# The first layer's weights loaded under the attention, and a new order of the layers' first group and of the change of layers

## The chip, the cores and the metric

One core of one Trainium2 chip runs the whole program. The metric is the device time in microseconds of one execution, the median of the runs shown.

## The reference, cut to what matters

```
mod = silu(c) @ wmod                      -> sa, ca, ga, sb, cb, gb (4 batches, 256 each)
h = layernorm(x) * (1 + ca) + sa          # x: 4 x 1024 x 256
x = x + ga * attention(h)                 # 4 heads of 64, full attention, RMS norm of q and k
h = layernorm(x) * (1 + cb) + sb
for l in range(2):                        # "the layers", weights of their own
    s = shift_token(h)                    # second half of the features from the token before
    q, k, v = split(s @ wqkv[l])          # 8 heads of 64
    q, k = l2norm(q) * q_scale[l], l2norm(k) * k_scale[l]
    q, k = rotary(q, k)
    h = h + local_attention(q, k, v) @ wo[l]     # windows of 128, own and previous
    a, g = split(layernorm(shift_token(h)) @ w1[l] + b1[l])
    h = h + (a * gelu(g)) @ w2[l] + b2[l]
x = x + gb * h
```

All products of weights are done in three passes over a high and a low part (the helper of lines 260 to 262), so each weight has to be split after it is loaded: the high part is a copy to the matmul's format on ScalarE (ACT), the low part is the difference of raw and high.

## The kernel before

Three blocks follow each other with a barrier between them: setup, attention, layers. In each block every engine has its own instruction list, written out by hand, and engines wait for each other on semaphores that count finished steps.

In the layers a unit is 128 tokens, a group g is four units; groups 0 to 7 are the first layer, 8 to 15 the second. The lists run over g from -1. In group -1 only the projections of group 0 are made. In every other group there are 12 rounds r of attention of two heads each (scores on TensorE, `minima` L1528 on VectorE (DVE), `exps` L1337 on ACT, `inverse` L1536 on DVE, `probabilities` L1737 on GpSimd (POOL), transposes and values on TensorE), and then 16 slots k. A slot holds the rest of the attention, one product of `qkv` for the group after (k 0 to 11), the feed-forward's `hidden` from k 4 and `outputs` from k 10. For the group after, ACT takes `squares` L1319, DVE `sums` L1495, the chain of 12 small instructions `norms` (L1501 and L89 to L94) and `rotated` (L1512, L1514), POOL `trig` (L1725 twice, L1730), which multiplies q and k with the table of angles `tab`. A product writes one of the banks P, A0 to A3; the scores use A0 to A3 as well.

Start of the layers: SyncE issues, after the barrier, the rows of units 0 and 1, `wqkv`, the rows of units 2 and 3, `tab`, six small loads of the scales, `w2`, `wo`, `w1`, the mask and `b2` (L1921 to L1933). The raw weights land in tiles that are free until the first group needs them. `first_wqkv`, `first_w2_wo` and `first_w1` are the splits. The low part of `w2` and `wo` is made on POOL in slot 5 of group -1, that of `w1` on DVE in slot 7, just ahead of the norms of units 0 and 1 in slot 8. POOL multiplies `tab` by the scales (L1711) first.

Change of layers: in group 7 SyncE's `take_q` loads the second layer's `wqkv` in six pieces of 256 KB into `ge`, `up`, `xn`, `base` (four, then two once the first two are split), and then `tab` and the scales again. In group 8 `take_rest` loads two pieces of `wo`, six of `w1` and three of `w2`, each batch after a wait for the splits of the last; the stores of group 7 and the shifts of group 8 stand behind it in the same queue. ACT makes the high parts in the rounds that W_Q, W_O and W_1 name (L1403, L1408, L1415), `piece_2` in slot 0; POOL makes the low parts of `wqkv`, `wo` and `w2` (L1771, L1775, L1781), DVE that of `w1` (L1618). The group's `moments` (L1551) need the shifted row, a transfer from SBUF to SBUF by SyncE (`shift`, L1844).

## Time and profile before

| | us |
|---|---|
| median of 3 runs | 2210.22 (2209.44 to 2210.82) |
| the profiled execution | 2207.61 |
| its span, first to last instruction | 2205.8 |
| attention's last stores, then first issue of the layers | 664.9 |
| busy: TensorE 1865.4 (85%), VectorE 1510.0 (68%), ScalarE 1186.2 (54%), GpSimd 996.6 (45%) | |

The span is the time from the first to the last instruction; the execution's own time is 1.8 us more, and the median of the runs 2.6 us above that. A busy share is an average over three blocks: what a stage is worth is read in its own stretch.

### The profile page before, as it was taken

Reading aid. Unit: us, or ns where it says so; the run is one execution under the profiler, and the core shown is the slowest. Engines: PE = TensorE matmul, PEld = TensorE weight load, DVE = VectorE, ACT = ScalarE, POOL = GpSimd, SP = SyncE. Lnnn points to the kernel's source line nnn. Section 1 sums busy time; section 2 is a strip of 40 time slices with the busy share of each in tenths; the row PEclk is TensorE's granted clock in tenths of the full one; section 3 lists DMA queues with packets and bytes.
Section 4 is the critical chain, followed back from the end, with each engine's and each line's share of the span. In section 5 each row is a group of like instructions: output and inputs, shape, how many; then the busy total and the mean of one; then the engine's idle time right before and its main releaser. Section 6 shows DMA issues by size and latency. Waiting matters only on the chain.

```text
span 2205.8 us, 36469 instructions
## 1 busy us (share of the span) xinstructions
PE 1865.4 (85%) x12941; PEld 1403.2 (64%) x12941; DVE 1510.0 (68%) x3723; ACT 1186.2 (54%) x2717; POOL 996.6 (45%) x788
## 2 busy tenths in 40 slices
PE   5569999999954799888899888987888999888986
PEld 3444444444433587776777867766776777777776
DVE  3678878877653685766867758584776857768673
ACT  0545545443433656656566565664656566565562
POOL 0325544647463444444444435543545445454451
PEclk7779999999976999999999999998999999999998
DMA  4000010101024000000000002011000000000000
GB/s 141 24 26 27 1 34 11 41 16 51 15 67 134 11 20 17 19 12 24 20 17 21 10 26 68 17 53 32 25 16 29 27 26 25 18 30 26 26 18 22
DMA packets 83407, 68.58 MB, mean 31 GB/s; under 512 B 10853, under 2 KB 79509, under 8 KB 83225
## 3 DMA queue, kind: packets, MB, share of 16 engines
q1 hardware_dynamic: 83224, 66.25, 9.7%
q8 instruction: 103, 1.69, 0.3%
q14 instruction: 80, 0.65, 0.1%
HBM read 45.22 MB, written 16.81 MB: 28 GB/s over the span
## 4 chain that ended last, share of the span: by engine, by line
PE 35%; DVE 18%; issue 6%; ACT 5%; DMA 2%; SPq 1%; POOL 1%; DVEq 0%; ACTq 0%; POOLq 0%
PE bank_O L1201 4%; PE bank_T L1189 3%; PE bank_A L260 3%; PE bank_A L262 3%; PE bank_P L260 3%; PE bank_A L261 3%; ACT l_sm L1337 3%; PE bank_P L261 2%; PE bank_P L262 2%; DVE l_t L1512 2%; PE bank_A L1178 2%; DVE l_sm L1528 2%; DVE l_u_lo L1594 2%; PE bank_T L1168 2%; PE bank_T L260 1%
## 5 line engine op out<-in xcount | busy, mean ns | idle before, releaser
L1737 POOL TENSOR_TENSOR l_sm<-l_sm,l_rinv 128x512 f32<-128x512 f32 (+1 forms) x256 | 250.1, 998 | 366.1 <-DVE l_rinv L1536 365.8
L1725 POOL TENSOR_TENSOR l_t<-l_qk,l_tab 128x512 f32<-128x512 f32 x128 | 170.1, 1350 | 328.8 <-DVE l_ss L1495 328.8
L1337 ACT ACTIVATE l_sm<-l_sm,l_nb 128x256 f32<-128x256 f32 (+1 forms) x512 | 248.1, 486 | 82.0 <-DVE l_nb L1528 81.8
L260 PE MATMUL bank_A<-l_f_hi,l_w_hi 128*114 128x256 f32 (+1 forms) x768 | 220.1, 287 | 3.7 <-DVE l_f_lo L1573 2.7
L262 PE MATMUL bank_A<-l_f_hi,l_w_lo 128*114 128x256 f32 (+1 forms) x768 | 216.0, 281 | 0.0
L261 PE MATMUL bank_A<-l_f_lo,l_w_hi 128*114 128x256 f32 (+1 forms) x768 | 215.8, 281 | 0.0
L1528 DVE CUSTOM_DVE_ANT_0 l_sm<-bank_A,l_mask 128x256 f32<-128x256 f32 (+1 forms) x512 | 177.1, 401 | 52.0 <-PE bank_A L1178 51.5
L1189 PE MATMUL bank_T<-ident,l_sm 128*128 128x128 f32 x960 | 149.1, 290 | 65.7 <-POOL l_sm L1737 34.4
L618 ACT ACTIVATE pr<-ps_S 128x1024 f32<-128x1024 f32 x128 | 130.7, 1023 | 125.4 <-PE ps_S L512 124.6
L1594 DVE TENSOR_TENSOR l_u_lo<-l_up,l_u_hi 114x256 fp32r<-114x256 f32 (+1 forms) x192 | 197.8, 1036 | 0.1
L861 POOL TENSOR_TENSOR acc<-acc,pr 128x1024 f32<-128x1024 f32 x64 | 155.8, 2435 | 51.0 <-ACT pr L618 46.5
L733 DVE TENSOR_REDUCE mxr<-ps_M 128x2 f32<-128x1024 f32 x128 | 154.8, 1210 | 32.3 <-PE ps_M L523 31.5
L1201 PE MATMUL bank_O<-l_pt,l_vt 128*64 128x128 f32 x1920 | 142.8, 288 | 35.9 <-DVE l_o_lo L1540 30.4
L1189 PEld LDWEIGHTS bank_T<-ident,l_sm 128*128 128x128 f32 x960 | 105.7, 145 | 101.1 <-issue 53.7
L1346 ACT COPY l_pt<-bank_T 128x512 f32<-128x512 f32 (+1 forms) x256 | 132.1, 560 | 65.3 <-PE bank_T L1189 65.3
L260 PE MATMUL bank_P<-l_wqkv_hi,l_h_hi 128*128 128x512 f32 x366 | 155.0, 423 | 9.6 <-DVE l_h_lo L1490 9.6
L1730 POOL TENSOR_TENSOR l_t<-l_qk,l_tab 128x1024 f32<-128x1024 f32 x64 | 157.0, 2453 | 0.0
L1201 PEld LDWEIGHTS bank_O<-l_pt,l_vt 128*64 128x64 f32 x1920 | 111.1, 139 | 64.5 <-DVE l_o_lo L1540 37.4
L1373 ACT ACTIVATE l_ge<-bank_A,cols 114x256 f32<-114x256 f32 (+1 forms) x192 | 90.9, 474 | 109.5 <-PE bank_A L262 102.8
L1178 PE MATMUL bank_A<-l_kt,l_qt 64*128 64x256 f32 (+1 forms) x1024 | 146.8, 403 | 1.5 <-DVE l_nb L1528 1.3
L1309 ACT COPY l_qk<-bank_P 128x512 f32<-128x512 f32 x122 | 71.6, 587 | 139.5 <-PE bank_P L262 139.5
L261 PE MATMUL bank_P<-l_wqkv_lo,l_h_hi 128*128 128x512 f32 x366 | 145.7, 398 | 0.0
(268 smaller groups left out, 5127.3 us busy)
## 6 DMA issues: line engine op xcount, KB each, us to landing
l_xs<-x_layers SPq DMA_DIRECT2D x64, 128.0 KB, 2.5
x<-in_x SPq DMA_DIRECT2D x8, 512.0 KB, 3.9
base_rows<-x SPq DMA_DIRECT2D x16, 256.0 KB, 2.1
x_layers<-x SPq DMA_DIRECT2D x16, 256.0 KB, 2.1
l_xs<-x_layers SPq DMA_DIRECT2D x64, 64.0 KB, 2.2
x_layers<-l_yb SPq DMA_DIRECT2D x32, 128.0 KB, 1.8
l_base<-base_rows SPq DMA_DIRECT2D x32, 128.0 KB, 3.1
out<-l_yb SPq DMA_DIRECT2D x32, 128.0 KB, 1.7
```

Of the source, the lines that this page charges most:

```text
L260: pe.matmul(out, a_hi, b_hi, start=(start and k == 0), stop=False)
L261: pe.matmul(out, a_hi, b_lo, start=False, stop=False)
L262: last = pe.matmul(out, a_lo, b_hi, start=False, stop=(stop and k == n - 1))
L1178: last = eng.matmul(halves[e][:, 0:P * windows(n)], qt[rows, n % QUAD, c, :], kt[rows, key_slots(n), c, :], start=True, stop=True)
L1189: last = eng.transpose(ps[:, q:q + P], sm[:, R % SS, e, P * v:P * v + P], ident[:, :])
L1201: last = eng.matmul(banks["O"][HD * e:HD * e + HD, P * c:P * c + P], vt[:, s, q:q + HD], pt[:, R % 2, 2 * e + v, :], start=(v == 0), stop= ...
L1337: eng.activation(row, row, ACT.Exp, bias=nb[:, R % SS, e:e + 1], scale=-1.0, accum_out=rsum[:, R % SS, e:e + 1]).then_inc(ex_ready, 1)
L1528: eng.tensor_tensor_reduce(sm[:, R % SS, e, 0:P * windows(n)], ps[:, 0:P * windows(n)], keep, 1.0, 3.0e38, ALU.add, ALU.min, nb[:, R % SS, ...
L1594: eng.tensor_tensor(u_lo[0:CS[j], m % US, :], up[0:CS[j], m % 3, :], u_hi[0:CS[j], m % US, :].bitcast(F32), ALU.subtract).then_inc(u_ready, 1)
L1725: eng.tensor_tensor(dst[:, :, :, lo:lo + H2], src[:, :, :, hi:hi + H2], table[:, :, 1, lo:lo + H2].unsqueeze(2).to_broadcast([P, 2, LH, H2 ...
L1730: eng.tensor_tensor(t1[:, n % 2].rearrange("p (a h) d -> p a h d", a=2), src, table[:, :, 0, :].unsqueeze(2).to_broadcast([P, 2, LH, HD]), ...
L1737: eng.tensor_tensor(row, row, rinv[:, R % SS, :].unsqueeze(2).to_broadcast([P, 2, P * windows(n)]), ALU.mult).then_inc(pn_ready, 1)
```

## The change

1. Four tiles of the attention (`x`, `qk`, `scr`, `m1`) are allocated outside both blocks. The layers place `qk`, `pt`, `sm`, `xn`, `ge`, `mask`, `b2`, `scales`, `gate`, `base` in them. SyncE loads `wqkv` (1536 KB), `w2` in two transfers (456 and 226 KB), `wo` (512 KB), the mask, `b2` of both layers and the first layer's scales there, 13 transfers, near the end of the attention; after the barrier are left the rows, `tab` and `w1`.

```diff
+            def load_layers():
+
+                t.wait_ge(done["qt"], 4 * A_HALVES)
+                t.wait_ge(done["xt"], 2 * A_HALVES)
+                t.wait_ge(h1_ready, 4 * A_HALVES)
+                t.wait_ge(scr_used, 6 * A_HALVES)
+                at = layer_tiles(share)
+                eng.dma_start(at["raw_q"], io["wqkv"][0].rearrange("(k p) n -> p k n", k=KC)).then_inc(early["wq"], 16)
...
+                if n == A_HALVES + 2 and j == 8:
+                    load_layers()
...
             load(0), load(1)
-            eng.dma_start(raw_q, io["wqkv"][0].rearrange("(k p) n -> p k n", k=KC)).then_inc(wq_loaded, 16)
-            load(2), load(3)
-            tables(0)
...
+            table(), load(2), load(3)
             for k in range(KC):
                 eng.dma_start(raw_1[k][:, 0:2 * HID], io["w1"][0, P * k:P * k + P, :]).then_inc(w1_loaded, 16)
...
+                if g == 1:
+                    w.wait_ge(tab_ready, 4)
+                    load_scales(eng, io, scales, tab_loaded, 1)
```

2. Group -1 and group 0. The low parts of `w2` and `wo` go from POOL (slot 5) to DVE (slot 4); the norms of units 0 and 1 come in slot 6, ahead of `first_w1`; the rotations in slots 7 and 9. Two of the `v` products move to rounds 0 and 2 of group 0. `tab` is multiplied in four quarters. The `trig` of units 1 and 3 waits until the DVE's norms chain is done.

```diff
+        LATE_V = ((2, 2), (3, 2))
+                        elif r in (0, 2):
+                            qkv(*LATE_V[r // 2])
...
-                    if k == 8 and ahead:
-                        norms(following // 2, also=first // 2 + 1 if g >= 0 else None)
+                    if k == 8 and ahead and g >= 0:
+                        norms(following // 2, also=first // 2 + 1)
...
-                    if g == -1 and k == 7:
-                        first_w1()
+                    if g == -1:
+                        if k == 4:
+                            first_w2_wo()
+                        if k == 6:
+                            norms(0)
+                        if k in (7, 9):
+                            rotated(k // 8)
+                        if k == 7:
+                            first_w1()
...
+                if n in (1, 3):
+                    w.wait_ge(chain, norms_done[n // 2])
+                        if r == 2 and g == 0:
+                            trig(3)
```

3. Change of layers. Pieces are split one round after another, the low parts of `wqkv` on DVE, `tab` in quarters in rounds 8 to 11; the three pieces of `w2` are loaded after group 8's values into `pt` and `base` and split in slots 7, 9 and 11.

```diff
-        W_Q = {2: (0, 1), 3: (2, 3), 8: (4, 5)}
-        W_O = {2: (0, 1)}
-        W_1 = {3: (0, 1), 7: (2, 3), 8: (4, 5)}
+        W_Q = {5: (0,), 6: (1,), 7: (2,), 8: (3,), 9: (4,), 10: (5,)}
+        W_O = {4: (0, 1)}
+        W_1 = {5: (0, 1), 9: (2, 3), 10: (4, 5)}
...
-                w.wait_ge(w2_ready, 2 if m < HC * GL else 2 + 3)
+                w.wait_ge(w2_ready, 2 if m < HC * GL else 2 + min(j // 2 + 1 + 3 * (q - 2 * GL), 3))
```

On DVE, and under it on POOL:

```diff
+                        if g == GL - 1:
+                            for i in W_Q.get(r - 1, ()):
+                                piece_q(i)
...
                         if g == GL - 1:
-                            for i in W_Q.get(r, ()):
-                                piece_q(i)
-                            if r == 10:
-                                tables(1)
+                            if r >= 8:
+                                tables(1, r - 8)
...
-                    if g == GL and k == 0:
-                        piece_2(0), piece_2(1), piece_2(2)
+                    if g == GL and k in (7, 9, 11):
+                        piece_2((k - 7) // 2)
```

On SyncE:

```diff
+            def take_2(i):
                 w.wait_ge(w1_ready, KC + 6)
-                for i in range(3):
+                w.wait_ge(pv_done, PAIRS * QUAD * (GL + 1))
...
                 quarter(3)
+                if g == GL:
+                    take_2(0)
                 shift(first + 3)
+                if g == GL:
+                    take_2(1), take_2(2)
```

## Rows read from the trace of the kernel before

**Rows 1.** Busy us by window: PE, weight load, DVE, ACT, POOL; clock, DMA share, GB/s.
```profile
722.20:815.90 93.70, 79.01 (x592) 65.90 (x593) 67.30 (x184) 52.75 (x141) 44.12 (x36) 0.95 0.04 10
...
1176.80:1268.00 91.20, 82.26 (x646) 69.45 (x645) 64.89 (x184) 55.60 (x142) 39.44 (x32) 1.00 0.06 18
...
1268.00:1357.20 89.20, 79.88 (x614) 66.92 (x614) 62.72 (x184) 53.92 (x142) 37.72 (x32) 1.00 0.06 19
...
1357.20:1455.80 98.60, 86.30 (x647) 72.16 (x646) 66.23 (x185) 59.16 (x148) 53.19 (x39) 0.95 0.15 45
...
1455.80:1564.30 108.50, 87.16 (x615) 72.62 (x614) 68.20 (x191) 60.39 (x153) 44.99 (x37) 0.89 0.14 43
```

**Rows 2.** Timeline, 664 to 695 us, several engines (start, duration, engine, line).
```profile
664.90 0.59 SPq L1838 DMA_DIRECT2D l_xs<-x_layers  x1
...
673.92 2.84 ACT L1385 CAST l_wqkv_hi<-l_qk 128x1536 fp32r<-128x1536 f32 x2 [15.85 <-DMA l_qk<-in_wqkv]
...
675.42 3.43 DVE L1606 TENSOR_TENSOR l_wqkv_lo<-l_qk,l_wqkv_hi 128x1536 fp32r<-128x1536 f32 x2 [13.39 <-ACT l_wqkv_hi L1385]
...
679.24 0.79 PE L260 MATMUL bank_P<-l_wqkv_hi,l_h_hi 128*128 128x512 f32 x1 [9.59 <-DVE l_h_lo L1490]
...
691.30 0.91 SPq L1933 DMA_DIRECT2D l_b<-in_b  x2
...
694.84 1.04 ACT L1389 CAST l_w_hi<-l_sm 114x1024 fp32r<-114x1024 f32 x1 [7.78 <-DMA l_sm<-in_w]
```

**Rows 3.** Timeline, 688 to 710 us, POOL and DVE taking turns.
```profile
688.02 2.50 POOL L1725 TENSOR_TENSOR l_t<-l_qk,l_tab 128x512 f32<-128x512 f32 x2 [2.08 <-DVE l_ss L1495]
...
690.47 2.34 POOL L1730 TENSOR_TENSOR l_t<-l_qk,l_tab 128x1024 f32<-128x1024 f32 x1
...
704.86 3.70 POOL L1730 TENSOR_TENSOR l_t<-l_qk,l_tab 128x1024 f32<-128x1024 f32 x1
...
706.29 3.71 DVE L1611 SCALAR_TENSOR_TENSOR l_w_lo<-l_kt,cols,l_w_hi 128x1364 fp32r<-128x1364 f32 x1
...
709.93 0.41 DVE L1490 TENSOR_TENSOR l_h_lo<-bank_T,l_h_hi 128x256 fp32r<-128x256 f32 x1
```

**Rows 4.** Timeline of DVE, 722 to 739 us, start of group 0: scores' minima, norms chain.
```profile
722.17 0.28 DVE L1528 CUSTOM_DVE_ANT_0 l_sm<-bank_A,l_mask 128x128 f32<-128x128 f32 x1
...
726.39 2.27 DVE L92 SCALAR_TENSOR_TENSOR l_ra<-l_rn 128x32 f32<-128x32 f32 x1
...
728.70 0.19 DVE L93 TENSOR_TENSOR l_ra<-l_ra,l_ss 128x32 f32<-128x32 f32 x1
...
738.57 0.42 DVE L1528 CUSTOM_DVE_ANT_0 l_sm<-bank_A,l_mask 128x256 f32<-128x256 f32 x1
```

**Rows 5.** Timeline of SyncE's queue, 470 to 640 us, neighbouring issues.
```profile
564.56 0.47 SPq L943 DMA_DIRECT2D xr<-in_x  x1
...
608.53 0.36 SPq L959 DMA_DIRECT2D x_layers<-x  x1
```

**Rows 6.** Timeline of groups 5 and 7; last row from tile l_tab.
```profile
1197.29 0.42 DVE L1546 TENSOR_TENSOR l_xs<-bank_T,l_xs 128x256 f32<-128x256 f32 x1 [0.34 <-PE bank_T L262]
...
1197.87 2.04 POOL L1737 TENSOR_TENSOR l_sm<-l_sm,l_rinv 128x512 f32<-128x512 f32 x2 [0.22 <-DVE l_rinv L1536]
...
1365.32 0.62 ACT L1403 CAST l_wqkv_hi<-l_ge 128x512 fp32r<-128x512 f32 x1 [2.15 <-DMA l_base<-in_wqkv]
...
1371.91 5.02 POOL L1737 TENSOR_TENSOR l_sm<-l_sm,l_rinv 128x512 f32<-128x512 f32 x4
...
DMA to landing us min/median/max: 5.8/6.8/7.7
```

**Rows 7.** Timeline of group 8: ACT, SyncE's queue, DVE.
```profile
1464.12 0.62 ACT L1408 CAST l_wo_hi<-l_ge 128x512 fp32r<-128x512 f32 x1 [3.31 <-DMA l_base<-in_w]
...
1484.25 8.98 SPq L1878 DMA_DIRECT2D x_layers<-l_yb  x2
...
1502.35 0.43 DVE L1551 BATCH_NORM_STATS2 l_st<-l_xs 128x6 f32<-128x256 f32 x1 [11.52 <-DMA l_xs<-l_xs]
```

More of the change, by code:

```diff
@@ L999, in sem @@
             return ctx.enter_context(nc.semaphore(f"l_{name}"))
+        at = layer_tiles(share)
+        qk, pt, sm, xn, ge, mask, b2, scales, gate, base, raw_q, raw_2, raw_o = (
+            at[n] for n in ("qk", "pt", "sm", "xn", "ge", "mask", "b2", "scales", "gate", "base", "raw_q", "raw_2", "raw_o"))
         wqkv = [sb(f"wqkv_{s}", [P, KC, 3 * INNER], F32R) for s in ("hi", "lo")]
@@ L1273, in _ @@
                         scores(*head(first, r)), scores(*head(first, r + 1))
-                    if k < HC and ahead:
+                    if k < HC and ahead and (following + k // 3, k % 3) not in LATE_V:
                         qkv(following + k // 3, k % 3)
@@ L1434, in _ @@
                         exps(*head(first, r))
+                        if g == 0 and r in (1, 3):
+                            qkv_out(*LATE_V[r // 2])
                         if r in (4, 6):
@@ L1453, in _ @@
                             pt_out(*head(first, r - 4)), pt_out(*head(first, r - 3))
-                    if k < HC and ahead:
+                    if k < HC and ahead and (following + k // 3, k % 3) not in LATE_V:
                         qkv_out(following + k // 3, k % 3)
@@ L1612, in first_w1, with piece_q @@
                                              in1=w1[0][:, k, :].bitcast(F32), op0=ALU.mult, op1=ALU.subtract).then_inc(w1_ready, 1)
+            def piece_q(i):
+                w.wait_ge(wq_hi, KC + i + 1)
+                k, s = divmod(i, 3)
+                c = slice(512 * s, 512 * s + 512)
+                eng.tensor_tensor(wqkv[1][:, k, c], AT_Q[i], wqkv[0][:, k, c].bitcast(F32), ALU.subtract).then_inc(wq_ready, 1)
             def piece_1(i):
@@ L1782, in piece_2 @@
                                   w2[0][0:n, 2 * i:2 * i + 2, :].rearrange("p c n -> p (c n)").bitcast(F32), ALU.subtract).then_inc(w2_ready, 1)
-            tables(0)
+            for i in range(4):
+                tables(0, i)
             for g in range(-1, GROUPS + 1):
@@ L1878, in store, with table, take @@
                 eng.dma_start(dst, yb[:, n % QUAD, :]).then_inc(y_stored[n % QUAD], 16)
-            def tables(l):
+            def table():
                 eng.dma_start(tab[:, :, :, :].rearrange("p t c d -> p t (c d)"), io["rope"].rearrange("t p c d -> p t (c d)")).then_inc(tab_loaded, 16)
-                for i, name in enumerate(("q_scale", "k_scale")):
-                    row = io[name][l:l + 1, :]
-                    eng.dma_start(scales[:, 2 * i, :], row.to_broadcast([P, HD])).then_inc(tab_loaded, 16)
-                    eng.dma_start(scales[:, 2 * i + 1, 0:HD // 2], row[:, HD // 2:HD].to_broadcast([P, HD // 2])).then_inc(tab_loaded, 16)
-                    eng.dma_start(scales[:, 2 * i + 1, HD // 2:HD], row[:, 0:HD // 2].to_broadcast([P, HD // 2])).then_inc(tab_loaded, 16)
-            def take(dst, src):
-                eng.dma_start(dst, src).then_inc(piece_loaded, 16)
+            def take(dst, src, loaded=piece_loaded):
+                eng.dma_start(dst, src).then_inc(loaded, 16)
             def take_q():
@@ L2004, in build @@
         cols = sb("cols", [P, 32])
+        share = {"x": sb("share_x", [P, 12 * D]), "qk": sb("share_qk", [P, 16 * D]),
+                 "scr": sb("share_scr", [P, 4 * D]), "m1": sb("share_m1", [P, 4 * D])}
+        early = {n: ctx.enter_context(nc.semaphore(f"l_{n}_loaded")) for n in ("wq", "wo", "w2", "par", "tab")}
         with ExitStack() as inner:
```

139 lines of the change are left out of this document (71 added, 68 removed).

## The prediction

> **What bounds the kernel now.** I read the page's busy shares first, then cut the span into stretches, since the change touches three short ones only. No engine is full over the span (TensorE 85%), and the rate differs by stretch. The layers' groups repeat: a group of the first layer takes 91.2 us when odd (group 5) and 89.2 us when even (group 6) [rows 1]. Three stretches stand out: 57.3 us from the layers' first issue (664.90) to group 0's first score minimum (722.17) [rows 2, 4]; group 7 with 98.6 us, 7.4 above its like; group 8 with 108.5 us, 19.3 above its like. Group 0, with no outputs of a group before it, takes 93.7, 4.5 above an even one [rows 1].
>
> In the first stretch the view of waits in time order shows loads. The layers' first issue is at 664.90; ACT can split wqkv from 673.92 after idling for its transfer; TensorE's first product runs at 679.24; then ACT idles again and begins w2 at 694.84, since all later loads stand in one queue [rows 2]. The second limit there is not a load: DVE and POOL take turns. POOL's third trig instruction takes 2.34 us alone and 3.70 beside DVE's split of w1; DVE's split, begun at 706.29, takes 3.71, ending 1.4 us after POOL's instruction ended at 708.56; DVE's next one, the low part of h for unit 3, starts at 709.93 [rows 3]. In group 0 the norms chain, which takes 0.19 us an instruction when POOL is idle (12 of them, some 2.6 us with the gaps), is stretched by trig of units 2 and 3: one link takes 2.27 us [rows 4].
>
> **The change part by part.** The profiled execution is 2207.6 us (span 2205.8), the median of the runs 2210.2; I subtract the sum from the median.
>
> *Loads under the attention.* 13 transfers are added to SyncE's queue of the attention. At the place where they come in, the queue issues nothing between 564.56 and 608.53 [rows 5], 44 us. The whole list of loads of the layers' start, which holds these 13 and more, took SyncE from 664.90 to 692.2 [rows 2]. So up to 27 us stand in 44 us of cover, and everything they wait for is long done. Cost 0; without the cover the next residual rows would be late and it would be up to 27. The second layer's scales are six issues more in group 1, behind which a store and a shift stand; their need is 20 us later: 0.
>
> *First products.* From ACT's split of wqkv to the first product the row distance is 679.24 - 673.92 = 5.32 us [rows 2]. ACT can now start at the barrier, 664.9, so TensorE starts at 670.2, 9.0 us earlier. The rows of units 0 and 1 are issued first, as before, and their transposes are no later than the weight's split.
>
> *Group -1, second half.* What is late next is DVE. The low parts of w2 and wo (1024, 512 and 1024 elements; wqkv's two of 1536 took 3.43, so 1.12 ns each [rows 2]) are 2.9 us on DVE, in the same moment as trig of unit 0 on POOL, 2.50 + 2.34 = 4.84 us [rows 3]. POOL starts it once tab has landed (issued after four issues of 0.6 us, at 667.4, landing 6.8 later [rows 6]) and is multiplied (2048 elements at POOL's 2.34 us per 1024 [rows 3], 4.7), 679.0. Taking turns from there, DVE ends w2 and wo at 686.8 instead of 683. Unit 2's products start at 687.2. Then sums and norms of units 0 and 1 (alone, as trig of unit 1 now waits for them) to 691.0. Now rotation of unit 0 (2.3), w1's two splits (1.53 each) and trig of unit 1 (4.84) are 10.2 us of turns: 701.4. The low part of h for unit 3 starts at 701.4 where it started at 709.93: 8.5 us earlier. Two v products fewer stand before the transposes of q and k (a v product is six instructions of at most 0.79 us [rows 2]), and the rotations are already done; the first minimum comes at 712.0 instead of 722.17 [rows 4]: 10.2 us earlier.
>
> *Group 0.* Trig of unit 2 still covers the norms' first 2 us; trig of unit 3 waits for them and for the first probabilities, and then shares turns with unit 2's rotation: it ends at 726 and unit 3's rotation at 728.4. The seventh minimum, at 738.57 before [rows 4], comes at about 729.2: 9.3 us earlier. The two late v products stand in TensorE's idle time behind the first scores. From there the group runs as before. Gain of both parts: 9.5 us. Ends: if turns fall badly at each of four meetings (one trig instruction each, 4 us in all) it is 5.5; if the subtractions did not take turns with POOL, 17.
>
> A rule of the Trainium skill stands behind that (SBUF — State Buffer, "Who interferes with whom"): a VectorE instruction with two SBUF inputs and a GpSimd one that reads SBUF hold a shared port pair one at a time, for the whole instruction. The trace agrees for the 3.70 and 3.71 us above. By it moving w2 and wo from POOL to DVE frees nobody; without it the start would gain 17.
>
> *Group 7.* POOL no longer makes wqkv's low parts; before, its four instructions put four probabilities in one queue (a wait of 2.15 us on ACT for the pieces, then 5.02 us of probabilities in a row) [rows 6]. Now ACT makes a high part in each of rounds 5 to 10, 6 x 0.62 = 3.7 us, and DVE six low parts of 512 elements, 0.57 each plus turns. Three of them stand before the first residual, at 1197.29 in group 5 [rows 6], which is 20.5 into the group; I put it at 22.2. A new wait is added: POOL's tables begin in round 8, and tab is issued only after the first two pieces are split, which is now round 7, about 18 us into the group. It lands 5.8 to 7.7 us later [rows 6], at 25 to 27, while the probabilities of round 8 would begin 21.1 into the group (1197.87). They stand behind it in POOL's list and start at 27.8. TensorE's need of them I estimate 4 us after their usual start (one instruction of 1.02 and the transposes ahead), so about 2.6 us remain. Sum: 91.2 + 1.7 + 2.6 = 95.5, 3 less than 98.6. Ends: the table hides (gain 5) or lands late (loss 1).
>
> *Group 8.* Before, ACT waited 3.31 us for the pieces in round 2, and the pieces of w2 held SyncE's queue: the stores' issue took 8.98 us, the shift came after them, and DVE idled 11.52 us for the shifted row [rows 7]. All three are gone: the pieces are asked for in round 4, after their landing at 1464.1, and w2's loads follow the shifts. What is late next is ACT in the rounds: eight copies of about 0.6, 4.7 us, of which little is slack there; I take 4.7. In slots 7 to 11 three POOL instructions of about 1.25 push trig of unit 1 into the norms of slot 8: between 0 (DVE's later steps are freed by as much) and 3 us, I take 1.5, nearer to the first. Sum 89.2 + 4.7 + 1.5 + about 0.6 for the second batch landing just in time = 96.0, 12.5 less than 108.5. Ends 8 and 16.
>
> All in all 9.5 + 3.0 + 12.5 = 25.0 us; 2210.2 - 25.0 = 2185 us. The steady groups (1 to 6, 9 to 15) have the same instructions.
>
> **The rivals.** *A: no turns at the start.* Then DVE's list runs through and 17 of the start's time come back: 25 + 7.5 = 32.5, 2178 us. For it: rows where DVE works beside probabilities without loss, but these read PSUM. Against it: [rows 3].
>
> *B: the queues bite at the change.* Tab lands late in group 7, POOL holds the probabilities 4 us longer, and DVE's added low parts take a turn each (six of 1 us) with half of it on the path: group 7 is 5 us slower than I say, group 8 gives 9 instead of 12.5. 25 - 8.5 = 16.5, 2194 us. For it: each low part now meets probabilities of 1 us each, and trig's turns in rows 3 show what that costs; against it: only the few that stand ahead of a minimum are on the path.
>
> *C: slower.* The 13 loads block SyncE in the attention. Their place is the queue ahead of h's stores and the residual rows; the price is what they take beyond the 44 us of cover. They must take 44 + 25 = 69 us to make the kernel slower, 2.5 times what the same loads and more took after the barrier. With, say, 75 us the time would be 2216. Rows 5 speak against it. The page's rule on DMA in the same chapter of the Trainium skill (SBUF — State Buffer, "SBUF: two separate sides") says that transfers don't slow engines; no row here shows it.
>
> *D: the change doesn't do what it says,* the barrier or an unseen wait keeps ACT until 673: only the change of layers gives, near B's time.
>
> **How the numbers follow.** Forecast (21 to 29 us gained) 0.50; A 0.17; B and D 0.23; between B and nothing 0.07; C 0.03. A measurement of this kernel can tell 0.2%, 4.4 us. Faster by more than that 0.93, within it 0.04, slower 0.03. The range from 2174 (36 gained: A with both other ends partly) to 2196 (14 gained: B and 2.5 more) leaves out about 2 in 10.
>
> **What would show it.** Right: first product at 670, first minimum of group 0 at 712, seventh at 729; DVE's splits of w2, wo and w1 with times above 1.15 and 1.53 beside POOL's trig; group 7 95.5 long with a wait of POOL's first quarter of tab for a DMA; group 8 96 long with no DVE idle of 11 us before a moment. Wrong: a group 0 that starts at 704 (A), a POOL wait of over 5 us in group 7 (B), or the layers' first issue after 665 (C).

## The result, and the profile after

The changed kernel takes 2197.47 us (median of 5 runs, 2195.9 to 2199.21), the kernel before 2210.2 (5 runs): a ratio of 0.9948, 95% interval [0.9934, 0.9963]. Forecast was 2185, with a range from 2174 to 2196. The change is faster, by 0.5%, but it gives 12.7 us instead of 25.

The profiled span falls from 2205.8 to 2195.7. The windows of the kernel after, cut at the first score minimum of each group, answer to [rows 1] (columns as there; PE is TensorE, DVE is VectorE, ACT is ScalarE, POOL is GpSimd, SPq is SyncE's queue): the start of the layers, group 0, group 7, group 8.

```profile
664.91:711.44 46.53, 26.47 (x96) 20.02 (x97) 30.51 (x32) 20.40 (x29) 21.07 (x12) 0.70 0.23 74
711.44:807.90 96.46, 83.57 (x602) 68.63 (x601) 66.56 (x183) 54.08 (x143) 48.68 (x37) 0.93 0.04 10
1349.80:1449.33 99.53, 84.37 (x646) 70.54 (x646) 69.37 (x191) 58.88 (x148) 45.23 (x36) 0.97 0.14 43
1449.33:1550.74 101.41, 84.28 (x618) 70.86 (x616) 68.68 (x191) 59.32 (x153) 45.36 (x37) 0.93 0.15 46
```

The layers' first issue is at 664.91, 664.90 before [rows 2], so the attention is the same. To the first minimum it takes 46.5 us instead of 57.3, group 0 96.5 instead of 93.7: together 8.0 gained. Group 7 is 99.5 (before 98.6), group 8 101.4 (before 108.5). Groups 1 to 6 take 541.9 (541.4 before), and from the end of group 8 to the end it is 645.0 us (641.5). Most of the last is not the change: in the experiments' profiles the same instructions take 642.0 to 645.7. Whether the 0.5 us between 641.5 and the lowest of these is the change was not tested. 8.0 - 0.9 + 7.1 - 0.5 - 3.5 = 10.2, the 10.1 of the spans.

*The start* came out at the moments that were forecast. In the timeline of the kernel after, 670 to 712 us, the reader sees the first product, the splits that VectorE took over, the split of w1, the low parts of h for units 2 and 3, and group 0's first minimum. They answer to [rows 2 to 4].

```profile
670.24 0.80 PE L260 MATMUL bank_P<-l_wqkv_hi,l_h_hi 128*128 128x512 f32 x1 [0.58 <-DVE l_h_lo L1535]
...
680.61 1.84 DVE L1655 TENSOR_TENSOR l_w_lo<-share_x,l_w_hi 114x1024 fp32r<-114x1024 f32 x1 [0.72 <-ACT l_w_hi L1432]
682.37 1.75 DVE L1657 TENSOR_TENSOR l_w_lo<-share_x,l_w_hi 113x512 fp32r<-113x512 f32 x1
684.05 3.36 DVE L1660 TENSOR_TENSOR l_wo_lo<-share_qk,l_wo_hi 128x1024 fp32r<-128x1024 f32 x1
687.33 0.41 DVE L1535 TENSOR_TENSOR l_h_lo<-bank_T,l_h_hi 128x256 fp32r<-128x256 f32 x1
...
697.51 3.71 DVE L1666 SCALAR_TENSOR_TENSOR l_w_lo<-l_kt,cols,l_w_hi 128x1364 fp32r<-128x1364 f32 x1
701.14 0.41 DVE L1535 TENSOR_TENSOR l_h_lo<-bank_T,l_h_hi 128x256 fp32r<-128x256 f32 x1
...
711.44 0.28 DVE L1574 CUSTOM_DVE_ANT_0 share_x<-bank_A,share_scr 128x128 f32<-128x128 f32 x1
```

Forecast 670.2, 687.2, 701.4 and 712.0; measured 670.24, 687.33, 701.14 and 711.44. The splits of w2 and wo take 6.95 us, added up, for 2.9 us of work; trig runs beside them on POOL (its three instructions take 6.3 us there instead of 4.84).

*Group 7* loses more than the plan saved. POOL waits in its list for the rope table (its rows, and SyncE's issue of the table behind two pieces):

```profile
1367.90 0.43 SPq L1939 DMA_DIRECT2D l_up<-in_wqkv  x1
1368.38 0.43 SPq L1936 DMA_DIRECT2D l_tab<-in_rope  x1
...
1377.63 2.48 POOL L1782 TENSOR_TENSOR l_tab<-l_tab,share_m 128x512 f32<-128x512 f32 x2 [5.50 <-DMA l_tab<-in_rope]
1380.07 2.04 POOL L1809 TENSOR_TENSOR share_x<-share_x,l_rinv 128x512 f32<-128x512 f32 x2
```

The table was issued 18.6 us into the group (forecast 18), but landed 9.2 us later (forecast 5.8 to 7.7). In the kernel before this same load stood behind the same two pieces and landed in 5.8 us; the 7.7 in [rows 6] is the table's other load, at the start. The probabilities behind it start 30.3 us into the group, where 27.8 was forecast and 21.1 is usual. The first residual came at 22.0 (forecast 22.2), the second at 38.6.

*Group 8* lost its idle VectorE [rows 7]: its first residual comes at 21.1 and its second at 31.6 (before 25.7 and 34.6), and VectorE's wait for the shifted row ahead of a moment, 11.52 us before, is 2.46 at most. But a new wait stands in slot 9. SyncE's queue first, then ScalarE, whose wait in front of the second piece's split counts the landings of the second (114 rows) and the third (113 rows) together:

```profile
1509.32 3.23 SPq L1908 DMA_DIRECT2D l_xs<-l_xs  x1
1512.59 0.48 SPq L1939 DMA_DIRECT2D share_qk<-in_w  x1
1513.12 0.40 SPq L1939 DMA_DIRECT2D share_m<-in_w  x1
...
1526.88 0.62 ACT L1464 CAST l_w_hi<-share_qk 114x512 fp32r<-114x512 f32 x1 [9.47 <-DMA share_m<-in_w]
```

The windows of the kernel after over that transfer say why it lasts. The last three columns are TensorE's clock, the busy share of the 16 DMA engines, and GB/s:

```profile
1510.00:1512.00 2.00, 2.00 (x16) 1.76 (x15) 0.45 (x2) 0.59 (x1) 0.00 (x0) 1.00 0.30 97
...
1518.00:1520.00 2.00, 0.19 (x2) 0.00 (x0) 1.97 (x2) 0.00 (x0) 2.00 (x2) 1.00 0.07 24
1520.00:1522.00 2.00, 0.00 (x0) 0.00 (x0) 1.73 (x9) 0.00 (x0) 0.30 (x1) 0.99 0.07 24
1522.00:1526.00 4.00, 3.00 (x9) 2.56 (x10) 1.83 (x6) 0.00 (x0) 0.00 (x0) 0.50 0.07 24
```

A share of 0.07 is one engine of 16, moving 24 GB/s; 226 KB at that rate are 9.6 us. In the first of these rows the first piece (114 rows, issued at 1508.16) is under way, with a share of 0.30 and 97 GB/s. TensorE, which was busy for 0.19 us between 1518 and 1522, is granted 0.50 of its clock (1.2 GHz) in the last row. The trace of before had the same transfer: issued at 1483.83, its landing ended a wait of ScalarE at 1498.44.

```profile
1483.83 0.37 SPq L1889 DMA_DIRECT2D l_base<-in_w  x1
...
1498.44 0.62 ACT L1421 CAST l_w_hi<-l_ge 114x512 fp32r<-114x512 f32 x1 [6.90 <-DMA l_base<-in_w]
```

### The profile page after: what moved, and what is told of

It is laid out like the page before. It is cut to its first block, busy times and chain, and to the rows that moved or that the text cites. A ratio compares the mean times of both kernels' runs of the same rounds, so it can differ in the third digit from the quotient of the medians.

```text
span 2195.7 us, 36483 instructions
## 1 busy us (share of the span) xinstructions
PE 1866.3 (85%) x12941; PEld 1401.6 (64%) x12941; DVE 1520.6 (69%) x3732; ACT 1185.2 (54%) x2717; POOL 992.3 (45%) x785
## 4 chain that ended last, share of the span: by engine, by line
PE 36%; DVE 19%; issue 7%; ACT 6%; DMA 1%; POOL 1%; DVEq 0%; SPq 0%; ACTq 0%; POOLq 0%
PE bank_O L1240 4%; PE bank_T L1228 3%; PE bank_P L260 3%; PE bank_A L260 3%; PE bank_A L262 3%; PE bank_A L261 3%; ACT share_x L1378 3%; DVE l_t L1558 3%; PE bank_P L262 3%; PE bank_P L261 3%; DVE share_x L1574 2%; PE bank_A L1217 2%; DVE l_u_lo L1639 2%; PE bank_T L1207 2%; PE bank_T L260 2%
## 5 line engine op out<-in xcount | busy, mean ns | idle before, releaser
L1809 POOL TENSOR_TENSOR share_x<-share_x,l_rinv 128x512 f32<-128x512 f32 (+1 forms) x256 | 251.1, 1002 | 374.1 <-DVE l_rinv L1582 373.8
L1797 POOL TENSOR_TENSOR l_t<-share_qk,l_tab 128x512 f32<-128x512 f32 x128 | 176.0, 1399 | 318.3 <-DVE l_ss L1540 312.9
L1378 ACT ACTIVATE share_x<-share_x,l_nb 128x256 f32<-128x256 f32 (+1 forms) x512 | 248.0, 487 | 80.9 <-DVE l_nb L1574 80.7
L1574 DVE CUSTOM_DVE_ANT_0 share_x<-bank_A,share_scr 128x256 f32<-128x256 f32 (+1 forms) x512 | 177.3, 401 | 57.4 <-PE bank_A L1217 56.9
L1228 PE MATMUL bank_T<-ident,share_x 128*128 128x128 f32 x960 | 148.7, 289 | 69.7 <-POOL share_x L1809 35.1
L1389 ACT COPY share_qk<-bank_T 128x512 f32<-128x512 f32 (+1 forms) x256 | 132.0, 559 | 68.3 <-PE bank_T L1228 68.3
L1240 PE MATMUL bank_O<-share_qk,l_vt 128*64 128x128 f32 x1920 | 141.0, 285 | 30.6 <-DVE l_o_lo L1586 30.6
L1802 POOL TENSOR_TENSOR l_t<-share_qk,l_tab 128x1024 f32<-128x1024 f32 x64 | 157.7, 2464 | 0.0
L1240 PEld LDWEIGHTS bank_O<-share_qk,l_vt 128*64 128x64 f32 x1920 | 109.4, 138 | 59.0 <-DVE l_o_lo L1586 37.4
L260 PEld LDWEIGHTS bank_A<-l_f_hi,l_w_hi 128*114 128x114 f32 (+1 forms) x768 | 136.6, 178 | 15.9 <-issue 12.7
```

The costliest lines, as they stand in the source:

```text
L260: pe.matmul(out, a_hi, b_hi, start=(start and k == 0), stop=False)
L1228: last = eng.transpose(ps[:, q:q + P], sm[:, R % SS, e, P * v:P * v + P], ident[:, :])
L1240: last = eng.matmul(banks["O"][HD * e:HD * e + HD, P * c:P * c + P], vt[:, s, q:q + HD], pt[:, R % 2, 2 * e + v, :], start=(v == 0), stop= ...
L1378: eng.activation(row, row, ACT.Exp, bias=nb[:, R % SS, e:e + 1], scale=-1.0, accum_out=rsum[:, R % SS, e:e + 1]).then_inc(ex_ready, 1)
L1574: eng.tensor_tensor_reduce(sm[:, R % SS, e, 0:P * windows(n)], ps[:, 0:P * windows(n)], keep, 1.0, 3.0e38, ALU.add, ALU.min, nb[:, R % SS, ...
L1797: eng.tensor_tensor(dst[:, :, :, lo:lo + H2], src[:, :, :, hi:hi + H2], table[:, :, 1, lo:lo + H2].unsqueeze(2).to_broadcast([P, 2, LH, H2 ...
```

## The experiments

The attention's end differs by execution: the layers' first issue is at 661.8 to 670.6 us in the profiles of kernels that share the attention. So beside each median stand the lengths of the stretches, all cut as above, from one profile of each kernel: "start" is from the layers' first issue to group 0's first minimum. Each ratio is to runs of the kernel before that were made beside that experiment; their medians were 2209.6 (w2_cut to both), 2209.7 (behind, and loads_after to late_none), 2206.9 (order_only, pool_w2, start_old, best) and 2209.0 (trig3_old, best2). So medians of different sets are compared by their ratios. Ratios whose intervals overlap don't tell two kernels apart; there the argument rests on the stretches.

| kernel | median us | ratio to before, 95% | start | group 0 | group 7 | group 8 |
|---|---|---|---|---|---|---|
| before | 2210.2 | | 57.3 | 93.7 | 98.6 | 108.5 |
| after | 2197.47 | 0.9948 [0.9934, 0.9963] | 46.5 | 96.5 | 99.5 | 101.4 |
| w2_cut | 2194.85 | 0.9930 [0.9917, 0.9943] | 46.5 | 96.5 | 99.2 | 98.8 |
| w2_early | 2199.14 | 0.9957 [0.9944, 0.9970] | 46.8 | 96.6 | 99.5 | 104.1 |
| tab_first | 2191.22 | 0.9915 [0.9902, 0.9928] | 45.7 | 96.3 | 93.4 | 100.4 |
| both | 2184.56 | 0.9895 [0.9881, 0.9910] | 45.6 | 96.3 | 93.5 | 97.6 |
| behind | 2182.07 | 0.9874 [0.9859, 0.9889] | 45.6 | 96.3 | 93.4 | 94.6 |
| order_only | 2197.77 | 0.9961 [0.9948, 0.9974] | 45.6 | 96.3 | 99.4 | 101.0 |
| loads_after | 2208.52 | 0.9995 [0.9984, 1.0006] | 57.7 | 95.8 | 99.8 | 100.9 |
| norms_free | 2198.91 | 0.9942 [0.9929, 0.9955] | 45.7 | 96.3 | 98.6 | 101.3 |
| late_none | 2194.96 | 0.9937 [0.9924, 0.9949] | 46.3 | 94.9 | 99.0 | 100.9 |
| pool_w2 | 2195.79 | 0.9954 [0.9941, 0.9967] | 47.6 | 95.7 | 100.4 | 101.5 |
| start_old | 2192.43 | 0.9933 [0.9919, 0.9948] | 44.8 | 92.6 | 99.9 | 104.1 |
| trig3_old | 2193.88 | 0.9936 [0.9921, 0.9952] | 46.5 | 94.9 | 99.3 | 101.1 |
| best | 2180.27 | 0.9887 [0.9871, 0.9903] | 46.3 | 94.8 | 93.4 | 94.8 |
| best2 | 2180.46 | 0.9864 [0.9843, 0.9885] | 45.7 | 92.5 | 93.4 | 96.7 |

**The late piece of w2: its shape.**

```
-                take(AT_2[i][0:n, :]..., io["w2"][1, ...]..., w2_loaded if i else piece_loaded)
+                for rows in ((slice(0, 112), slice(112, n)) if i == 2 else (slice(0, n),)):
+                    take(dst[rows], piece[rows], w2_loaded if i else piece_loaded)
```

(Here dst and piece are the two operands of the line above. Cut: the wait of ScalarE for these loads goes from 64 to 80, for the one transfer more.)

> Only the load of layer 1's third w2 piece (113 rows) is changed: it goes as two transfers, 112 rows and 1 row. Theory S (shape): the 113-row transfer is served by one DMA engine, so that it alone needs some 14 us; with 112 rows it lands about 4 to 5 us after its issue, ScalarE's wait of 9.47 us ahead of piece_2(1) goes, the ninth group takes 93 to 94 us instead of 101.4, and the time falls by 7 to 9 us, to about 2189.5. Rival Q (queue): the load is late because it stands behind the shifts in SyncE's queue and shares the rings with other transfers; then it still lands 11 to 14 us after its issue and the time stays at 2197 (within 2).

The shape is the cause of the late landing. In the windows and timeline of this kernel the 112-row load shares 1514 to 1515 us with the end of the 114-row one, and ScalarE's wait before the second piece is 0.39 us:

```profile
1514.00:1515.00 1.00, 1.00 (x9) 0.95 (x8) 0.98 (x2) 0.59 (x1) 1.00 (x3) 1.00 0.72 203
1515.00:1516.00 1.00, 1.00 (x9) 0.96 (x8) 0.46 (x2) 0.77 (x2) 1.00 (x1) 1.00 0.56 184
...
1518.16 0.62 ACT L1464 CAST l_w_hi<-share_qk 114x512 fp32r<-114x512 f32 x1 [0.39 <-DMA share_m<-in_w]
```

But the group gained 2.6 us, not 8, and the time is 2194.85 instead of the 2189.5 of theory S. What then held the group is in the same kernel's timeline of POOL, VectorE and ScalarE:

```profile
1513.00 1.29 POOL L1837 TENSOR_TENSOR l_w_lo<-share_qk,l_w_hi 114x512 fp32r<-114x512 f32 x1 [7.75 <-ACT l_w_hi L1464]
...
1514.95 2.73 POOL L1797 TENSOR_TENSOR l_t<-share_qk,l_tab 128x512 f32<-128x512 f32 x2
...
1517.64 2.38 DVE L1549 TENSOR_SCALAR l_ss<-l_mv 128x2 f32<-128x2 f32 x1
...
1524.73 0.41 ACT L1422 CAST l_u_hi<-l_up 113x256 fp32r<-113x256 f32 x1 [5.58 <-DVE l_up L1633]
```

POOL's low part of piece 0 stands ahead of trig of the next group's second unit and waits 7.75 us for ScalarE. So trig starts 65.3 us into the group (57.8 in group 6), meets the norms chain of slot 8 (0.16 to 0.20 us an instruction in group 6, here up to 2.38), and ScalarE waits 5.58 us for VectorE.

**The same load, only earlier.**

```
                 quarter(2)
+                if g == GL:
+                    take_2(0), take_2(1), take_2(2)
                 shift(first + 2)
                 quarter(3)
-                if g == GL:
-                    take_2(0)
                 shift(first + 3)
-                if g == GL:
-                    take_2(1), take_2(2)
```

> All three loads of layer 1's w2 pieces are issued ahead of shift(first + 2) instead of around shift(first + 3); shapes unchanged. Theory W (the wait is the cost): issued near 1496 instead of 1508 to 1513 they have landed by about 1510 although the last still needs 14 us; ScalarE's wait of 9.47 us goes and the ninth group takes about 93.5 us: 7 to 9 us less, about 2189.5. Rival P (the pieces' own work in slots 7, 9 and 11 is the cost, three copies on ScalarE and three subtractions on POOL beside the trig): the group keeps at least 6 of its 9 extra us, and the time falls by under 3 us.

Both were wrong: the group grew to 104.1. SyncE's queue and VectorE in this kernel:

```profile
1504.88 0.38 SPq L1939 DMA_DIRECT2D share_m<-in_w  x1
1507.50 6.35 SPq L1899 DMA_DIRECT2D l_xs<-l_xs  x1
1513.89 5.13 SPq L1908 DMA_DIRECT2D l_xs<-l_xs  x1
...
1522.29 0.43 DVE L1597 BATCH_NORM_STATS2 l_st<-l_xs 128x6 f32<-128x256 f32 x1 [12.28 <-DMA l_xs<-l_xs]
```

Behind the one-engine load the next two issues take 6.35 and 5.13 us (about 0.65 and mostly 0.54 to 0.99 in the other groups), and VectorE waits 12.28 us for the shifted row. It is the picture of [rows 7]. The wait was moved, not removed.

Why the shift suffers most can be read from the windows of the same kernel:

```profile
1507.00:1509.00 2.00, 2.00 (x18) 1.91 (x16) 0.85 (x2) 1.70 (x3) 2.00 (x2) 1.00 0.41 144
1510.00:1521.00 11.00, 7.09 (x49) 6.19 (x47) 0.01 (x1) 3.26 (x6) 1.04 (x2) 1.00 0.08 25
```

The shift moves 127 rows (63.5 KB), and where it runs by itself it shows one engine's share too: 0.07 over 1503 to 1506 us in the kernel after. Here the 113-row load and a shift are both outstanding, and the share stays at that of one engine for 11 us. 226 and 63.5 KB at 24 GB/s are 12 us by estimate, so the two moved one after the other. While both 114-row pieces were under way with the 113-row one, the rate was 144 GB/s, six times 24.

**The table first.**

```
                 if g == GL - 1:
-                    take_q()
                     w.wait_ge(trig_ready, 3 * UL)
                     table()
+                    take_q()
```

> In the eighth group SyncE issues the rope table's load ahead of the six wqkv pieces instead of behind them. Theory T (the late landing is the cost): the table has landed before round 8, POOL's wait of 5.50 us goes, probabilities(8) start about 22 to 24 us into the group instead of 30.3, the group takes 93 to 95 us instead of 99.5, and the time falls by 5 to 6 us, to about 2192. Rival U (the four quarters of the table's multiplication, in rounds 8 to 11 of POOL's order, delay the probabilities by themselves, some 5 us of POOL work): at least half of the 7 us stays, and the time falls by under 3 us. Rival V (the pieces, now behind the table, land late and take over as the wait): no gain.

Theory T to the number: 93.4 us, 6.1 less. Rows of SyncE's queue, POOL and the window of group 7 in this kernel: the table is issued 2.4 us into the group, lands 5.7 us later, and POOL's first quarter follows the probabilities without a wait.

```profile
1348.89 0.43 SPq L1936 DMA_DIRECT2D l_tab<-in_rope  x1
...
1368.76 2.95 POOL L1782 TENSOR_TENSOR l_tab<-l_tab,share_m 128x512 f32<-128x512 f32 x2
1371.67 2.49 POOL L1809 TENSOR_TENSOR share_x<-share_x,l_rinv 128x512 f32<-128x512 f32 x2
...
1346.51:1439.95 93.44, 82.46 (x646) 69.39 (x645) 70.95 (x191) 58.70 (x148) 46.60 (x36) 1.00 0.15 46
```

**All three.**

> The table's load first, the w2 loads ahead of shift(first + 2), and the 113-row load cut in 112 and 1. If the two waits are separate costs of groups eight and nine, the gains add: 13 to 15 us below the changed kernel, about 2183.5. If they are one (the second hides behind the first), it is no better than the better of the single edits, about 2189.5.

The gains of the two groups add, 6.0 and 3.8 us by their lengths; the medians differ by 12.9, just under the forecast's 13. This run also separates the load's shape from its place: the w2 loads are issued as early as in w2_early, but with the 113 rows cut the next two issues take 0.66 and 2.16 us instead of 6.35 and 5.13, the longest wait for a shifted row around them is 3.77 us instead of 12.28, and group 8 takes 97.6 us instead of 104.1.

**The order on POOL.** In both kernels here the three piece_2 calls of POOL stand behind its trig instead of ahead of it; "behind" has the table first and the cut load too, "order_only" nothing else.

```
-                    if g == GL and k in (7, 9, 11):
-                        piece_2((k - 7) // 2)
                     if k in (1, 5, 7) and g >= 0:
                         ...
                         trig(following + {4: 0, 7: 1, 12: 2, 14: 3}[k])
+                    if g == GL and k in (7, 9, 11):
+                        piece_2((k - 7) // 2)
```

> The table's load first and the 113-row load cut, as in the last two runs, and besides POOL makes w2's three low parts behind the trig instructions of slots 7, 9 and 11 instead of ahead of them. With the load cut, the ninth group still took 98.8 us, 6.4 more from its fourth residual on than an even group; in its trace trig of the next group's second unit starts 7.5 us late, behind the first low part, which waited for ScalarE. Theory O (order on POOL): with trig ahead that lag goes, the norms of slot 8 are not held, and the group takes 92 to 93.5 us; time 2178 to 2180. Rival P (the pieces' own 3.8 us on POOL and 1.9 us on ScalarE): it stays above 97 and the time near 2184 to 2185.

> The changed kernel with one edit: POOL makes w2's three low parts behind the trig instructions of slots 7, 9 and 11; the 113-row load stays whole and late, the table stays behind the pieces. Theory (two lags side by side in the ninth group): ScalarE still waits for the load until about 77 us into the group, so the group keeps 99 to 101.4 us and the time 2195 to 2197.5. Rival (the lags stand one behind the other): the 4.2 us that the order gave beside the cut load come here too, group 97, time 2193.

From w2_cut to behind group 8 falls by 4.2 us (98.8 to 94.6), but the table's place was changed too, and that alone took 1.0 off group 8 (101.4 to 100.4 in tab_first). So with the load cut the order is worth 3.2 to 4.2 us, without it 0.4 (101.4 to 101.0). Rows of POOL and the window of group 8 in the first kernel, then ScalarE's wait in the second:

```profile
1505.11 2.73 POOL L1797 TENSOR_TENSOR l_t<-share_qk,l_tab 128x512 f32<-128x512 f32 x2 [0.46 <-DVE l_ss L1540]
1507.79 2.42 POOL L1802 TENSOR_TENSOR l_t<-share_qk,l_tab 128x1024 f32<-128x1024 f32 x1
1510.13 1.51 POOL L1837 TENSOR_TENSOR l_w_lo<-share_qk,l_w_hi 114x512 fp32r<-114x512 f32 x1
...
1444.70:1539.33 94.63, 82.59 (x617) 69.55 (x616) 68.16 (x191) 59.62 (x153) 45.65 (x37) 0.96 0.17 50
```

```profile
1522.12 0.62 ACT L1464 CAST l_w_hi<-share_qk 114x512 fp32r<-114x512 f32 x1 [8.58 <-DMA share_m<-in_w]
```

So two lags lay side by side: one repair alone gives 2.6, the other 0.4, and both with the table's new place give 6.8, of which at most 1.0 is the table's. The theory of order_only holds for the group (101.0); its time, 2197.77, is 0.3 above what it said. Theory O gets the direction and most of the size, but its 93.5 us and its 2180 were not reached; of the 5.4 us over an even group's 89.2, 2.4 are there by the first residual (20.9 against 18.5 in group 6). I put these down to ScalarE's copies in the rounds; no run tests it.

**What the early loads are worth.** The block load_layers() goes out of the attention, and its 13 loads back among the first ones of the layers, in the order of before.

> The changed kernel with its 13 early loads put back behind the attention's end, in SyncE's order of the kernel before. All else (splits on VectorE, late v products, norms first) stays. Theory L (the loads are the gain at the start): ScalarE starts its first split 9 us later, w2 and wo near 695, and the first minimum comes 8 to 11 us later counted from the end of the attention (46.5 us in the changed kernel, so 55 to 57); time about 2207. Rival M (the start is bound by VectorE and POOL taking turns, so most of the loads' lead is absorbed): 2 to 5 us later, about 2201.

Theory L, with 57.7 us of start (0.7 above its range) and 2208.52. The windows of start and group 0 in this kernel:

```profile
662.54:720.20 57.66, 26.39 (x96) 19.95 (x97) 26.64 (x31) 20.29 (x29) 19.59 (x12) 0.68 0.36 119
720.20:816.00 95.80, 83.80 (x602) 68.70 (x601) 66.51 (x184) 53.97 (x143) 48.66 (x37) 0.93 0.04 10
```

Start and group 0 take 153.4 us against 151.0 before: without early loads, the rest of the start's edits cost 2.4 us.

There is a rival to moving all 13 loads that was not tried. The first layer's w2 has a 113-row load as well, and in the kernel before it stands among the loads of the start. SyncE's queue in the kernel before, the 113-row load and the load of wo behind it:

```profile
675.96 2.25 SPq L1927 DMA_DIRECT2D l_sm<-in_w  x1
678.25 10.60 SPq L1928 DMA_DIRECT2D l_pt<-in_f_wo  x1
```

ScalarE could begin w2 only at 694.84 [rows 2], 18.9 us after that issue, and w1's loads went out behind the 10.60 us. From 684 to 688 the DMA share was 0.07, at 23 GB/s. Under the attention the same two issues take 2.35 and 10.31 us and nothing waits for them. How much of the loads' gain the cut into 112 rows and 1 would have given by itself is open.

**The rest of the start, one by one.**

```
-        LATE_V = ((2, 2), (3, 2))
+        LATE_V = ()
...
```

> The changed kernel with the v products of units 2 and 3 in their old place in group -1 instead of in group 0. Theory: two products of six instructions stand ahead of the transposes again, the first minimum comes 2 to 5 us later and group 0 is up to 2 us shorter: time 2198 to 2201. Rival (VectorE, not TensorE, is what is late there): the first minimum stays within 1 us and group 0 gets shorter by up to 2.7 us, so that the time falls to about 2195.5.

The rival: the first minimum stayed (46.3), group 0 took 1.6 less, and the median is 2194.96 (the ratios' intervals overlap, so the stretches decide). TensorE did not need the relief in group -1, and the two products cost in group 0.

```
-                if n in (1, 3):
-                    w.wait_ge(chain, norms_done[n // 2])
```

> The changed kernel without the wait of trig(1) and trig(3) for the norms of units 0 and 2. Theory N (turns): the norms' small instructions again each stand beside a POOL instruction, and the seventh minimum of group 0 comes 1 to 4 us later: time 2198.5 to 2201. Rival F (POOL's idle 9.96 us and the probabilities pushed by trig(3) are the dearer): 1 to 3 us earlier, about 2195.5; group 0's first residual comes at 23 us into the group instead of 25.7.

Neither: start and group 0 take 142.0 us together, and the first residual stays late. Kernels with an untouched start show 142.0 (tab_first, both, behind, order_only) or 142.9 to 143.3 (after, w2_cut, w2_early). So the wait is worth nothing that these profiles show, and the late residual of group 0 is not its doing (25.5 us into the group here, 25.7 after, 23.0 before).

```
-                        if k == 4:
-                            first_w2_wo()
...
+                    if g == -1 and k == 5:
+                        first_w2_wo()
```

> The changed kernel with w2's and wo's low parts back on POOL (slot 5 of group -1, as before the change). Theory (VectorE and POOL take turns there, so that it frees nobody): the first minimum stays 45.5 to 47.5 us behind the layers' first issue and the time within 2 us of 2197.5. Rival (VectorE's list bounds the start and its 2.9 us of subtractions count): the first minimum comes at 43 to 44, time about 2194.5. Rival (POOL's list bounds it): 49 to 50 us, time about 2200.5.

(The first two lines are VectorE's, the others POOL's.) Start and group 0 take 143.3 against 142.0 to 143.3: moving these splits to VectorE freed nobody, as turns would have it. The first minimum, at 47.6, lies 0.1 outside the theory's range and far from both rivals.

```
-                        if r == 2 and g == 0:
-                            trig(3)
...
-                    if k in (4, 7, 12, 14) and ahead and (g >= 0 or k < 14):
+                    if k in (4, 7, 12, 14) and ahead:
```

(Cut: trig(3)'s wait for the norms goes with it; that wait was worth nothing in norms_free.)

> The changed kernel with trig(3) back in group -1 (slot 14) instead of behind the first score pairs of group 0. Of the 5.6 us that the old form of the start gave back, the late v products were 1.8, the norms wait 1 and w2 on POOL nothing clear. Theory T3 (the probabilities of group 0's first pairs stand behind trig(3) on POOL): group 0 takes 93.5 to 95 us instead of 96.5, the first minimum stays at 46 to 47 us behind the layers' first issue, time about 2195.5. Rival (trig(3) then stretches the norms chain, the whole of what it saves): start and group 0 together stay within 0.7 us of 143.0, time 2197.5.

Theory T3, at 94.9 us for group 0: trig(3) among group 0's first probabilities costs 1.6. Start and group 0 together are 141.3, outside the rival's 0.7 around 143.0 and 0.7 below the lowest of the kernels with an untouched start.

**The old start with early loads.** The last four edits together, and norms and rotations of units 0 and 1 back in slots 8 to 10.

> The changed kernel with its early loads, but with everything else of the start as in the kernel before: w2's and wo's low parts on POOL, norms and rotations of units 0 and 1 in slots 8 to 10, trig(3) in group -1, no late v products, no waits of trig for norms. The run with the loads put back behind the attention had first minimum and group 0 together 2.5 us above the kernel before. Theory E (the loads are all of the start's gain, the other edits cost 2 to 3 us): first minimum at about 46 us, group 0 at 93.7, time about 2195. Rival G (the edits pay only once the loads are early, since VectorE and POOL are then what is late): first minimum at 49 to 52, time 2199 to 2202.

Theory E, and more: 44.8 + 92.6 = 137.4 us, 5.6 below the changed kernel and 4.6 below the 142.0 of four kernels with the same start. Windows of start and group 0 in this kernel:

```profile
661.83:706.60 44.77, 26.86 (x104) 20.05 (x104) 27.33 (x29) 21.59 (x31) 27.18 (x16) 0.78 0.24 77
706.60:799.20 92.60, 78.50 (x592) 65.31 (x593) 66.41 (x183) 52.61 (x141) 43.45 (x36) 0.94 0.04 10
```

The early loads (with tab's four quarters and its place ahead of the last rows, which stayed) give 151.0 - 137.4 = 13.6 us. The late v products and trig(3), 1.6 each by group 0, explain about 3.2 of the 4.6 to 5.6 that the other edits take back. The place of norms and rotations was not tried by itself, so the other 1.4 to 2.4 us stay open. So does another thing: group 8 took 104.1 here.

**Put together.**

> Table's load first, 113-row load cut, POOL's low parts of w2 behind trig, the v products of units 2 and 3 back in group -1 and trig(1), trig(3) without their wait for norms. If the start's two edits are worth what their single runs showed (group 0 shorter by 1.6, first minimum earlier by up to 0.8), this is 2 us below the version without them: about 2180. If they only pay one by one, it stays at 2182.

> Early loads, table's load first, 113-row load cut, POOL's low parts of w2 behind trig, and everything else of the start as in the kernel before. If the old start's 5.6 us stand by themselves, start and group 0 take 137.4 us, groups 7 and 8 93.4 and 94.6, and the time is 2175 to 2177.5. If the 2.7 us by which the ninth group was longer with the old start (104.1 against 101.4) come with it, it is 2178 to 2180.

They are 1.1 and 1.4% faster than the kernel before and, by the ratios, 0.6 and 0.8% faster than the changed one. They can't be told from each other: their intervals overlap. For best, the 0.9 us less at the start than in behind (141.1 against 142.0) is a single profile's, and the times don't settle its two cases. best2 falls on its second case: group 8 is 2.1 us longer than in behind. best2 has the better start (138.2 against 141.1) and the longer group 8 (96.7 against 94.8), as start_old had. Its first residual comes 2 us later there than in best; in the two timelines ScalarE's exponentials drift apart by 0.3 us near 20 us into the group, and then a pair of probabilities on POOL starts 21.5 us into the group in best and 23.4 in best2. What decides that stays open.

## Why the prediction was wrong

**Loads under the attention, first products: right.** The 13 issues took SyncE 18.7 us (564.71 to 583.45), inside the 44 us of cover: the next store of the attention is issued at 608.53 in both kernels, and the layers' first load at 664.9 in both. 9.0 us forecast for the first product, 9.0 measured. Rival C is refuted, and D with it.

**Group -1, second half: right in its times, wrong in what it was worth.** Each forecast moment came within 0.6 us. But the step says that the two v products out of the way and the early rotations bring the first minimum forward; start_old shows that the minimum would have come at 44.8 us, earlier than the 46.5, without any of these edits, and in late_none it came at 46.3 with the v products back in front of it. I priced the edits together and never asked what the loads alone would give. They give 13.6 us; the rest takes 4.6 to 5.6 back. Rival A (no turns) is refuted by the splits' times; its price of 17 us at the start has no working in the prediction, and no run shows it. One reading of the rows was wrong too: the prediction says that ScalarE idled for w2 until 694.84 because all later loads stand in one queue. The loads of w2 had been issued by 678.2 (675.96 plus 2.25 us); by the share of 0.07 from 684 to 688 what lasted was the 113-row transfer, the same shape that failed the forecast in group 8.

**Group 0: the failed step is "From there the group runs as before".** The seventh minimum came at 729.45 (forecast 729.2), but the residual stood 25.7 us into the group instead of 23.0. trig(3) (1.6) and the v products (1.6) sit on the path there; for what follows the seventh minimum the prediction put both at nothing. Gain 8.0 instead of 9.5.

**Group 7: the term of the table was mis-sized.** The sum was 91.2 + 1.7 + 2.6. The first two held (with the table's wait gone the group takes 93.4); the third was 6.6 (99.5 - 92.9). The landing took 9.2 us where I allowed at most 7.7 [rows 6]. The same load in the same place landed in 5.8 us before, and in 7.2 to 9.4 in every changed kernel that keeps it behind the pieces; with the table first it is 5.6 to 5.8. Why the pieces cost it more than before stays open (the two stores of the group now follow it directly, where six loads of scales stood between; no run tests that). And the "about 2.6 us remain" rested on an estimate that TensorE needs the probabilities 4 us later than they usually come. They came 9.2 us late and 6.6 showed. This is the first half of rival B, the table that lands late; tab_first took away 6.1 us of it.

**Group 8: the failed step is "about 0.6 for the second batch landing just in time", with "I take 1.5" for POOL's order beside it.** The prediction took the landing of w2's loads as free, because the waits in [rows 7] that they caused were going; I never looked at how long the transfer itself takes. The rows of before had it: 14.6 us from issue to ScalarE. Here it held ScalarE for 9.47 us. Under it lay the second lag, the low part ahead of trig on POOL: forecast 0 to 3 us, worth 3.2 to 4.2 once the load was cut. From the fourth residual to the end the group took 42.6 us where group 6 takes 33.6: 9.0 more, and I had allowed 2.1. The rounds were cheaper than my 4.7: 2.6 by the first residual, 3.2 by the second. 89.2 + 3.2 + 9.0 = 101.4 instead of 96.0.

The Trainium skill has the rule that I should have used (DMA: Bandwidth & Descriptors, "Why a DMA increments its semaphore by 16 and not by 1"): a transfer is spread over the largest number of engines up to 16 that divides the outermost dimension of both sides. By that rule, as an estimate, 113 rows go over one engine, 114 over six, 112 over 16. The trace agrees: a share of 0.07 at 24 GB/s for 113 rows; 0.41 at 144 GB/s, six times that, while the 114-row pieces ran (in w2_early, with the 113-row one beside them); up to 0.72 at 203 GB/s for 112 rows, with the end of another transfer in it.

The prediction's rule of turns between VectorE and GpSimd, from the Trainium skill (SBUF — State Buffer, "Who interferes with whom"), held at the start. The trace agrees with 6.95 us for 2.9 us of subtractions, and pool_w2 shows its practical side: a subtraction moved between the two engines moved no time.

Misses in sum: 1.5 at the start, 3.9 in group 7, 5.4 in group 8, 10.8 of the 12.3 between 25 and 12.7. The other 1.5 is a balance: groups 1 to 6 (0.5) and the stretch behind group 8 (3.5) took more, and the medians differ by 2.6 more than the two profiled spans.

## What to carry to other kernels

Before a transfer is called hidden, read how long it lasts from issue to landing and at what share of the DMA engines; a share of one sixteenth is a shape to mend (here 113 rows cut into 112 and 1), and moving its issue earlier in a busy queue only moved the wait to whatever was queued behind it. Where two lags lie side by side, one repair shows almost nothing: ask of every wait what would end just behind it. And when a change has one strong part and several reorderings, price the strong part alone first; here it gave 13.6 us, and the reorderings took 4.6 to 5.6 back.

## What the runs showed of the hardware

- A 226 KB load of 113 rows used one DMA engine's worth of share (0.07) at 24 GB/s, about 14 us from issue to use; as 112 rows and 1 it was done within 5.4 us of its issue.
- Right behind such a load, issues on the same queue were slow: 10.60 us (wo's load at the start of the kernel before) and 10.31 (the same under the attention), 8.98 (two stores, before, [rows 7]), 6.35 and 5.13 (a shift's two transfers, w2_early). With the load cut these last two were 0.66 and 2.16.
- A transfer of 127 rows (the shift) used one engine's worth of share as well, and with the 113-row load outstanding the two together stayed at one engine's worth (0.08, 25 GB/s, for 11 us).
- The end of the attention lies anywhere from 661.8 to 670.6 us in profiles of kernels that share it, while groups 2 to 5 repeat within 0.11 us. Group 6 does not (89.2 to 91.3), and start and group 0 of kernels with the same start range over 1.3 us. So stretches of the trace tell edits of about 1.5 us apart, which medians of 5 runs do not, but no smaller ones.
